# Group-norm and convolution chain, one core: statistics summed by TensorE, edge rows set by ScalarE, x1's rows stored ahead of x(2)'s loads

## Chip, cores and metric

One core of one Trainium2 chip. The metric is the device time in microseconds of one execution, median of the runs.

## What is computed

x has 8 images of 16 channels, 128 x 128, f32. Four residual steps follow each other:

```python
x = x + conv3x3(gn(x), w0) + b0                    # zero padding
x = x + newton_schulz(gn(x), 5)                    # each channel a 128x128 matrix
x = x + circular_conv3x3(gn(x), w2)                # the reference writes it with FFTs
x = x + conv3x3_cut(gn(x), K)                      # last row and column masked to 0

def gn(v, G=8, eps=1e-05):                         # 8 groups of 2 channels
    g = v.reshape(B_, G, C_ // G, H_, W_)
    m = jnp.mean(g, axis=(2, 3, 4)); s = jnp.var(g, axis=(2, 3, 4))
    return (g - m) / jnp.sqrt(s + eps)

X = W.T / (norm1 * norminf)                        # newton_schulz
for _ in range(5):
    X = X @ (2 * I - W @ X)
```

## The kernel before

The steps are called A (conv w0), B (Newton-Schulz), C (conv w2) and D (conv K).

**Convolutions.** An image is cut into NBLK = 22 windows of 8 rows x 16 channels = 128 partitions, each giving 6 output rows (96 partitions). The stationary matrix has 3 x 96 columns (one block per horizontal tap); its f32 values and those of the window are split in a high and a low fp32r part, so that a group of four windows is nine matmuls of 512 columns (`conv_group`, L815). The 22 windows are six groups (SPLIT_G). The normalization goes into the weights (1/sd, `conv_weights` L649 to L658) and into the high parts (minus the mean, ScalarE, `high_parts` L699); the low parts come from VectorE (`low_parts` L664), or from GpSimd (`low_parts_pool` L672) after ScalarE has shifted the window by L702. The output leaves PSUM by `conv_out` (ScalarE, L841).

**Statistics of a window tile** (A and D) go in four steps. `win_stats_1`: bn_stats and two bn_aggr on VectorE, one for the first 21 windows, one for the last, into mv; then `shares` (L566, L567) weights the two per partition. `win_mean` on TensorE (L710) sums over the partitions of a group with one f32 matmul of a single column against same_group. `win_stats_2` on VectorE (L602 to L631): copy of the mean, deviation, square, plus variance, `shares` again; then the values for the edges (L608), the negative mean (L609), the first window's row above the image (L614), the output's bias, the last window's row below it (L631). `win_var` (L717) sums; `win_stats_3` adds eps, ScalarE takes the root (L1026), `win_stats_4` is a reciprocal and a Newton step (L530 to L534), and `win_weights` follows. Almost every one of these operations waits for the one before it through a semaphore (class Chain). Rows B and C (the same statistics in row layout, x1 and x2) use `row_stats_1` to `row_stats_4` (L725 to L755), with `row_mean` (L760) and `row_var` (L767) on TensorE giving 16 columns, which VectorE adds in pairs (L735, L747).

**B** holds image b in x1 (128 rows x 16 channels x 128) and works on 4 channels at a time, two streams (s = 0, 1) in turn. A cycle per image has SLOTS = 24 slots; a slot is one product of a stream: TensorE (L916/L920, or L925 to L929, or L934), then ScalarE zh (L1038), then VectorE zl (L1124). Into the slots the other work is written by hand, `pe_cycle`, `act_cycle`, `dve_cycle`, `pool_cycle`, `sp_cycle`: which conv group (FILL), which step of which statistic. Cycle i computes B of image i, C of i-1, D of i-2 and A of i+3. Every engine runs its own list in order. Cycles 2 and 3 are a loop on the device, 0, 1 and 4 to 7 are written out; cycles 2, 3 and 4 are full, 5 and 6 have no A.

**Prologue.** x(0) and x(1) are loaded by three queues (every third window each: SyncE, ScalarE, GpSimd). A of 0 and 1 is done by `first_convs`; x1's rows of image 0 are gathered window by window from A's output (`rows_from_windows` L341, L345), again by the three queues. SyncE's list is: constants, taps A, x(0), taps C and D, bias, x(1), the ten loads of x(2) (L312, L317), its rows of x1, x(3), the store of x1(1) (L354); then, as cycle 0 begins, the copy x1 to x2 (L380) and the load of the next x1 (L370). VectorE's list is: stationary matrix of A, `first_convs` with x(2)'s `win_stats_1` at its end, row statistics of x1(0), the sums for B's norms (L1145, L1147), their scales, x(2)'s `win_stats_2`, the end of the row statistics, cycle 0. GpSimd forms DN (L1354) and DS (L1365), the operands of B. In cycle 0 VectorE also builds the stationary matrices of C and D (`stationary` L1216, L1223) at slots 3 to 8 (KEEP_Q).

## Time and profile before

| what | value |
|---|---|
| median of 3 runs | 738.2 us (738.06 to 3227.26) |
| profiled execution | 734.13 us, span 732.3 us |
| TensorE busy, mean granted clock | 611.9 us, 0.952 |
| VectorE, ScalarE, GpSimd busy | 538.9, 383.3, 197.7 us |

The profile is of one execution, whose own time stands beside its span. Times in it are microseconds from the span's start. PE is TensorE's matmul, PEld its weight load, DVE VectorE, ACT ScalarE, POOL GpSimd, SP SyncE; SPq, ACTq are issues of DMAs by these engines. L12 is line 12 of the kernel. The stages by their first product of a cycle: prologue to 70.5, cycles from 70.5, 150.3, 229.1, 308.0, 388.9, 467.4, 540.5 and 612.3, tail from 665.

### The profile page before, as it was taken

Reading aid. Unit: us, or ns where it says so; the run is one execution under the profiler, and the core shown is the slowest. Engines: PE = TensorE matmul, PEld = TensorE weight load, DVE = VectorE, ACT = ScalarE, POOL = GpSimd, SP = SyncE. Lnnn points to the kernel's source line nnn. Section 1 sums busy time; section 2 is a strip of 40 time slices with the busy share of each in tenths; the row PEclk is TensorE's granted clock in tenths of the full one; section 3 lists DMA queues with packets and bytes.
Section 4 is the critical chain, followed back from the end, with each engine's and each line's share of the span. In section 5 each row is a group of like instructions: output and inputs, shape, how many; then the busy total and the mean of one; then the engine's idle time right before and its main releaser. Section 6 shows DMA issues by size and latency. Waiting matters only on the chain.

```text
span 732.3 us, 11055 instructions
## 1 busy us (share of the span) xinstructions
PE 611.9 (84%) x3752; PEld 509.1 (70%) x3752; DVE 538.9 (74%) x1304; ACT 383.3 (52%) x559; POOL 197.7 (27%) x285
## 2 busy tenths in 40 slices
PE   0746788885999998989999999998979897988785
PEld 0535667775777777877877777777877787886454
DVE  4757885768688877978787968875787678856570
ACT  0430553743376745756566737673447445753472
POOL 5104222402124232512243312423032303200232
PEclk9986799998999999999999999999989998999899
DMA  6697011094049733593139614433063315134415
GB/s 171 78 116 206 7 28 55 22 193 145 30 107 97 236 87 90 74 269 77 38 87 193 174 47 102 139 121 86 18 187 101 87 38 142 66 86 121 99 48 114
DMA packets 89415, 76.52 MB, mean 104 GB/s; under 512 B 6464, under 2 KB 81568, under 8 KB 86536
## 3 DMA queue, kind: packets, MB, share of 16 engines
q1 hardware_dynamic: 84692, 72.69, 42.8%
q0 software_dynamic: 1344, 1.62, 1.1%
q10 hardware_dynamic: 3332, 1.61, 1.0%
q8 instruction: 26, 0.43, 0.3%
q14 instruction: 21, 0.17, 0.1%
HBM read 38.14 MB, written 24.25 MB: 85 GB/s over the span
## 4 chain that ended last, share of the span: by engine, by line
PE 42%; DVE 33%; ACT 9%; issue 6%; DMA 5%; SPq 3%; POOL 1%; ACTq 0%; DVEq 0%
PE conv_ps L815 23%; DVE zl L1124 7%; PE z L925 4%; PE z L934 4%; PE z L929 3%; PE z L927 3%; ACT zh L1038 3%; DVE stB L725 3%; DVE bn_D L587 2%; PE z L920 2%; DVE d_C L664 2%; ACT d_A L699 2%; DMA x<-out_C 1%; DVE bn_A L587 1%; DMA rows_dram<-x 1%
## 5 line engine op out<-in xcount | busy, mean ns | idle before, releaser
L1124 DVE SCALAR_TENSOR_TENSOR zl<-z,zh 128x1024 fp32r<-128x1024 f32 x128 | 154.4, 1219 | 77.4 <-ACT zh L1038 75.5
L925 PE MATMUL z<-zh 128*128 128x256 f32 x512 | 154.0, 301 | 12.0 <-DVE zl L1124 12.0
L1038 ACT ACTIVATE zh<-z 128x1024 fp32r<-128x1024 f32 x128 | 130.1, 1019 | 64.4 <-PE z L929 43.3
L929 PE MATMUL z<-zh,zl 128*128 128x256 f32 x512 | 147.0, 287 | 0.0
L927 PE MATMUL z<-zl,zh 128*128 128x256 f32 x512 | 147.0, 287 | 0.0
L815 PE MATMUL conv_ps<-d_C,w_C 128*96 128x512 f32 (+1 forms) x540 | 134.7, 399 | 13.8 <-POOL d_C L852 6.9
L815 PEld LDWEIGHTS conv_ps<-d_C,w_C 128*96 128x96 f32 x540 | 86.5, 172 | 43.7 <-issue 8.9
L925 PEld LDWEIGHTS z<-zh 128*128 128x128 f32 x512 | 100.4, 196 | 21.1 <-DVE zl L1124 17.7
L927 PEld LDWEIGHTS z<-zl,zh 128*128 128x128 f32 x512 | 100.3, 196 | 1.4
L929 PEld LDWEIGHTS z<-zh,zl 128*128 128x128 f32 x512 | 100.1, 195 | 0.0
L815 PE MATMUL conv_ps<-d_A,w_D 128*96 128x512 f32 (+1 forms) x378 | 91.8, 390 | 9.7 <-DVE w_D L657 9.7
L815 PE MATMUL conv_ps<-d_A,w_A 128*96 128x512 f32 (+1 forms) x378 | 89.2, 384 | 8.9 <-DVE w_A L657 7.4
L672 POOL TENSOR_TENSOR d_A<-win_D,d_A 128x512 fp32r<-128x512 f32 (+1 forms) x42 | 48.2, 1150 | 117.4 <-ACT win_D L702 117.1
L815 PEld LDWEIGHTS conv_ps<-d_A,w_D 128*96 128x96 f32 x378 | 58.7, 166 | 30.4 <-DVE w_D L657 7.4
L815 PEld LDWEIGHTS conv_ps<-d_A,w_A 128*96 128x96 f32 x378 | 58.1, 164 | 29.9 <-DVE w_A L657 6.5
L841 ACT ACTIVATE out_C<-conv_ps,col_C 96x512 f32<-96x512 f32 (+1 forms) x42 | 27.2, 648 | 65.0 <-PE conv_ps L815 64.9
L852 POOL TENSOR_TENSOR d_C<-d_C,ones_all 128x8 fp32r<-128x8 f32 (+1 forms) x96 | 22.6, 266 | 131.4 <-DVE d_C L664 131.4
L672 POOL TENSOR_TENSOR d_A<-win_A,d_A 128x512 fp32r<-128x512 f32 (+1 forms) x30 | 33.3, 1110 | 83.2 <-ACT win_A L702 83.2
L841 ACT ACTIVATE out_A<-conv_ps,col_A 96x512 f32<-96x512 f32 (+1 forms) x36 | 23.3, 648 | 58.7 <-PE conv_ps L815 58.5
L1354 POOL TENSOR_TENSOR DN<-x,tB 128x512 f32<-128x512 f32 x32 | 35.8, 1123 | 61.1 <-DVE devB L742 36.9
L841 ACT ACTIVATE out_D<-conv_ps,col_D 96x508 f32<-96x508 f32 (+1 forms) x42 | 27.1, 646 | 44.2 <-PE conv_ps L815 44.0
L1137 DVE SCALAR_TENSOR_TENSOR x<-z,sx,x 128x256 f32<-128x256 f32 x64 | 27.8, 477 | 29.5 <-PE z L934 29.5
(193 smaller groups left out, 923.1 us busy)
## 6 DMA issues: line engine op xcount, KB each, us to landing
x<-x_dram SPq DMA_DIRECT2D x14, 1024.0 KB, 7.4
win_C<-rows_dram SPq DMA_DIRECT2D x40, 256.0 KB, 4.3
rows_dram<-x SPq DMA_DIRECT2D x32, 256.0 KB
win_D<-out_C SPq DMA_DIRECT2D x7, 1056.0 KB, 6.8
y<-out_D SPq DMA_DIRECT2D x42, 168.0 KB, 3.9
win_A<-x SPq DMA_DIRECT2D x40, 160.0 KB
x_dram<-out_A SPq DMA_DIRECT2D x30, 192.0 KB, 2.4
win_D<-out_C SPq DMA_DIRECT2D x14, 160.0 KB, 5.9
```

The lines of the kernel that those rows point to most:

```text
L672: pool.tensor_tensor(c.d[:, 1, k0:k0 + kn, 1:W + 1], c.win[:, k0:k0 + kn, :], c.d[:, 0, k0:k0 + kn, 1:W + 1].bitcast(f32), ALU.subtract).t ...
L815: ins = pe.matmul(conv_ps[g % 2][0:OP, 0:kn, :], c.w[:, wp, dx * OP:(dx + 1) * OP], c.d[:, dp, k0:k0 + kn, dx:dx + W], start=n == 0, stop= ...
L841: act.activation(c.out[:, k0:k0 + kn, 0:wn], conv_ps[g % 2][0:OP, 0:kn, 0:wn], ACT.Identity, bias=col(c, OUTB, rows=OP)).then_inc(c.s_out, 1)
L852: return pool.tensor_tensor(out, in_, ones, ALU.mult)
L925: pe.matmul(z[s][:, m, :], zh[s][:, m, 0:128], zh[s][:, m, :], start=False, stop=True, skip_group_check=True)
L927: pe.matmul(z[s][:, m, :], zh[s][:, m, 0:128], zl[s][:, m, :], start=False, stop=True, skip_group_check=True)
L929: ins = pe.matmul(z[s][:, m, :], zl[s][:, m, 0:128], zh[s][:, m, :], start=False, stop=True, skip_group_check=True)
L934: ins = pe.matmul(z[s][:, m, 128:256], z4[s][:, m, 0:128], z4[s][:, m, 128:256], start=False, stop=True, skip_group_check=True)
L1038: act.activation(zh[s][:, :, :], z[s][:, :, :], ACT.Copy, scale=ROOT[j]).then_inc(s_zh[s], 1)
L1124: dve.scalar_tensor_tensor(zl[s][:, :, :], z[s][:, :, :], ROOT[j], zh[s][:, :, :].bitcast(f32), ALU.mult, ALU.subtract).then_inc(s_zl[s], 1)
L1137: ins = dve.scalar_tensor_tensor(x2[:, cs, :], z[s][:, GC * a:GC * (a + 1), 128:256], sx[:, g:g + 1], x2[:, cs, :], ALU.mult, ALU.add)
L1354: pool.tensor_tensor(DN[:, NMAT * ch:NMAT * (ch + 1), :].rearrange("p (g a) w -> p g (a w)", a=GC), x1[:, NMAT * ch:NMAT * (ch + 1), :].re ...
```

## The change

1. Sums. `shares` is gone. The constants hold four matrices minus_share (128 x 128 each, instead of one same_group and four columns); `win_mean` is two accumulating matmuls (first 21 windows, last window) and `win_var` four (variance and squared deviation of each). The results are negative, so that the negative mean comes out directly. VectorE's `win_stats_1` ends at bn_aggr; `win_stats_2` is copy, deviation, square, bias, edge values; `win_stats_4` squares and multiplies in one operation. `row_mean` is two matmuls of 8 columns and `row_var` four; VectorE's additions in pairs (L735 becomes a copy, L747 goes) and L742 go.
2. Edge rows. VectorE's L614 and L631 go; ScalarE does both inside `high_parts` (group 0 and group 5), each followed by a wait for itself.
3. Prologue, queues. SyncE: x(1) right after x(0), then the rows of x1, then x(2), x(3). Taps C, D and bias: ScalarE's queue, between x(0) and x(1).
4. Stationary matrices of C and D: by GpSimd, after its memsets and ahead of its loads of x(1), instead of VectorE in cycle 0.
5. x(2)'s statistics: `win_stats_1` after the scales of the norms; `win_stats_2`, `_3`, `_4` in slots 1, 2, 4 of cycle 0; the end of the first row statistics in slot 0; `win_mean` and `win_var` before slots 2 and 3; A2's conv groups in slots 6, 8, 9, 11, 13, 15, its high parts in 3, 4, 5, 7, 8, 10.
6. The last window of D of image 7 has no step of its own in VectorE's tail.

The core of the diff:

```diff
-K_RES = K_SEL + 128
+K_RES = K_SEL + 4 * 128
...
+    for j, share in enumerate(shares):
+        c[:, K_SEL + 128 * j:K_SEL + 128 * (j + 1)] = -share[:, None] * same_group
...
         def win_stats_2(dve, c, b):
-            link(dve.tensor_copy(col(c, MEAN), misc_ps[:, c.stat:c.stat + 1]))
+            link(dve.tensor_copy(col(c, NEG), misc_ps[:, c.stat:c.stat + 1]))
             dev2 = col(c, DEV, 2, rows=rows)
-            link(dve.tensor_scalar(dev2, c.mv[0:rows, :, 0], col(c, MEAN, rows=rows), None, ALU.subtract))
-            link(dve.tensor_tensor(dev2, dev2, dev2, ALU.mult))
-            link(dve.tensor_tensor(dev2, dev2, c.mv[0:rows, :, 1], ALU.add))
-            shares(dve, link, c, b, col(c, DEV, rows=rows), col(c, DEV + 1, rows=rows))
-            link(dve.tensor_scalar(col(c, ADD, 2), edge_drop, col(c, MEAN), None, ALU.mult))
-            link(dve.tensor_scalar(col(c, NEG), col(c, MEAN), -1.0, None, ALU.mult))
...
+            link(dve.tensor_scalar(dev2, c.mv[0:rows, :, 0], col(c, NEG, rows=rows), None, ALU.add))
+            dve.tensor_tensor(dev2, dev2, dev2, ALU.mult).then_inc(c.s_stat, 1)
+            if is_D(c):
+                dve.tensor_scalar(col(c, OUTB), col(c, NEG), -1.0, None, ALU.mult)
             else:
-                last_window(dve, c).then_inc(c.s_fix, 1)
+                dve.tensor_tensor(col(c, OUTB, rows=OP), bias[:, :], col(c, NEG, rows=OP), ALU.subtract)
+            dve.tensor_scalar(col(c, ADD, 2), minus_drop, col(c, NEG), None, ALU.mult).then_inc(c.s_fix, 1)
...
+        def edge_rows(act, c, b, k, j):
+            act.activation(c.win[:, k, :], c.win[:, k, :], ACT.Identity, bias=col(c, ADD + j),
+                           scale=edge_keep[:, j:j + 1]).then_inc(c.s_edge, 1)
+            act.wait_ge(c.s_edge, at(2, b, j + 1))
...
         def high_parts(act, c, b, g):
+            if g == 0 and not is_C(c):
+                edge_rows(act, c, b, 0, 0)
+            if g == NG - 1 and not is_C(c):
+                edge_rows(act, c, b, NBLK - 1, 1)
...
         def win_var(pe, c, b):
-            pe.matmul(misc_ps[:, c.stat + 1:c.stat + 2], same_group[0:rows, :], col(c, SUM, rows=rows),
-                      start=True, stop=True).then_inc(c.s_sum, 1)
+            out = misc_ps[:, c.stat + 1:c.stat + 2]
+            for a in range(2):
+                pe.matmul(out, minus_share[j + a][0:rows, :], c.mv[0:rows, a, 1:2], start=a == 0, stop=False)
+                ins = pe.matmul(out, minus_share[j + a][0:rows, :], col(c, DEV + a, rows=rows),
+                                start=False, stop=a == 1)
+            ins.then_inc(c.s_sum, 1)
...
         @block.sync
             load_x(sp, 0, ON_SP)
-            load_taps(sp, cC)
-            load_taps(sp, cD)
-            sp.dma_start(bias[:, :], bass.AP(tensor=b0.tensor, offset=b0.offset,
-                                             ap=[[0, OUT_ROWS], [1, C], [1, 1]])).then_inc(s_wrest, 16)
             load_x(sp, 1, ON_SP)
+            for g in range(NG):
+                rows_from_windows(sp, g, ON_SP)
             load_x_rows(sp, 2)
-            for g in range(NG):
-                rows_from_windows(sp, g, ON_SP)
             load_x_rows(sp, 3)
...
         @block.gpsimd
+            pool.wait_ge(s_cst, 16)
+            pool.wait_ge(s_wrest, 16 * 3)
+            for n, c in enumerate((cC, cD)):
+                for dy in range(TAPS):
+                    stationary(pool, c, dy, cD.scaled[:, :], s_toep_pool, (2 * TAPS - 1) * n)
             load_x(pool, 1, ON_POOL)
...
         @block.scalar
             load_x(act, 0, ON_ACT)
+            load_taps(act, cC)
+            load_taps(act, cD)
...
             load_x(act, 1, ON_ACT)
```

## Rows read from the trace of the kernel before

**Rows 1.** The page, parts 1 and 4: busy time; chain by engine.

```profile
PE 611.9 (84%) x3752; PEld 509.1 (70%) x3752; DVE 538.9 (74%) x1304; ACT 383.3 (52%) x559; POOL 197.7 (27%) x285
...
PE 42%; DVE 33%; ACT 9%; issue 6%; DMA 5%; SPq 3%; POOL 1%; ACTq 0%; DVEq 0%
```

**Rows 2.** By stage: length, busy (instructions) of engines, clock, DMA share, GB/s.

```profile
70.50:150.30 79.80, 65.29 (x391) 56.63 (x392) 59.02 (x129) 39.69 (x56) 24.92 (x23) 0.89 0.16 42
...
308.00:388.90 80.90, 74.49 (x472) 61.93 (x471) 65.52 (x160) 48.97 (x73) 24.70 (x33) 0.98 0.54 118
```

**Rows 3.** Waits of TensorE in the full cycle 308.0 to 388.9.

```profile
PE conv_ps L815 <- DVE w_D L657: 1.8, 1, 1.8
...
PE misc_ps L717 <- DVE col_A L567: 1.0, 1, 1.0
PE misc_ps L760 <- DVE stB L725: 0.8, 1, 0.8
```

**Rows 4.** Waits of TensorE in cycle 0, 70.5 to 150.3.

```profile
PE misc_ps L760 <- DVE stB L725: 3.6, 1, 3.6
...
PE conv_ps L815 <- DVE w_C L657: 2.4, 1, 2.4
```

**Rows 5.** Timeline, prologue: start, length, engine, line, operation [idle before].

```profile
39.12 0.45 ACT L841 ACTIVATE out_C<-conv_ps,col_A 96x256 f32<-96x256 f32 x1
...
40.37 1.81 DVE L664 SCALAR_TENSOR_TENSOR d_A<-win_A,col_A,d_A 128x512 fp32r<-128x512 f32 x3 [0.37 <-ACT d_A L699]
...
45.70 3.32 DVE L587 BATCH_NORM_STATS2 bn_A<-win_C 128x6 f32<-128x384 f32 x7 [3.53 <-DMA win_C<-x]
...
54.29 2.71 DVE L725 BATCH_NORM_STATS2 stB<-x 128x6 f32<-128x256 f32 x8 [4.21 <-DMA x<-out_C]
...
57.51 4.79 PE L815 MATMUL conv_ps<-d_A,w_A 128*96 128x512 f32 x18
...
76.04 2.36 DVE L1124 SCALAR_TENSOR_TENSOR zl<-z,zh 128x1024 fp32r<-128x1024 f32 x2
```

**Rows 6.** Timeline of SyncE's queue: issue start and length.

```profile
25.79 3.99 SPq L312 DMA_DIRECT2D win_C<-x  x8
...
31.48 11.99 SPq L341 DMA_DIRECT2D x<-out_C  x7
43.51 0.70 SPq L345 DMA_DIRECT2D x<-out_C  x1
44.27 10.33 SPq L312 DMA_DIRECT2D win_A<-x  x8
...
68.49 0.37 SPq L370 DMA_DIRECT2D x<-x_dram  x1
```

**Rows 7.** A stretch of four microseconds, columns as in rows 2.

```profile
30.00:34.00 4.00, 4.00 (x21) 2.95 (x20) 2.27 (x13) 1.27 (x2) 1.75 (x3) 1.00 1.28 113
```

**Rows 8.** The view of DMAs: one issue, KB each, us to landing.

```profile
y<-out_C POOLq DMA_DIRECT2D x7, 48.0 KB, 3.0
```

**Rows 9.** The page, part 5: GpSimd's smallest tensor_tensor, mean ns second.

```profile
L852 POOL TENSOR_TENSOR d_C<-d_C,ones_all 128x8 fp32r<-128x8 f32 (+1 forms) x96 | 22.6, 266 | 131.4 <-DVE d_C L664 131.4
```

**Rows 10.** Timeline beside GpSimd's DS; durations of L566, min/median/max.

```profile
69.40 1.08 DVE L604 TENSOR_SCALAR col_A<-mv_A,col_A 128x2 f32<-128x2 f32 x1
69.42 4.04 POOL L1365 TENSOR_TENSOR DS<-DN,scl 128x512 f32<-128x512 f32 x4 [6.71 <-DVE scl L1165]
...
L566 DVE TENSOR_TENSOR col_A<-col_A,cst x8: 158/160/962, 17.8 to 434.6; 128x1 f32<-128x1 f32 x8
```

**Rows 11.** Groups by line: busy us, mean ns.

```profile
L614 DVE TENSOR_SCALAR win_D<-win_D,cst,col_D 128x128 f32<-128x128 f32 x7 | 2.4, 346 | 0.9 <-DVE col_D L609 0.8
...
L1223 DVE TENSOR_TENSOR base_C<-base_C,scaled_C 128x288 f32<-128x288 f32 x2 | 1.8, 899 | 0.1
...
L1216 DVE TENSOR_TENSOR scaled_C<-compact_C,cst 128x288 f32<-128x288 f32 x2 | 0.9, 448 | 0.0
```

**Rows 12.** Timeline of TensorE's weight loads.

```profile
349.82 0.50 PEld L916 LDWEIGHTS z<-cst,DS 128*128 128x128 f32 x4
```

More of the change, by code:

```diff
@@ L111, in build @@
         ident = cst[:, K_IDENT:K_IDENT + 128]
-        same_group = cst[:, K_SEL:K_SEL + 128]
-        share = cst[:, K_SHARE:K_SHARE + 4]
+        minus_share = [cst[:, K_SEL + 128 * j:K_SEL + 128 * (j + 1)] for j in range(4)]
         residual = cst[:, K_RES:K_RES + WN]
@@ L616, in win_stats_2 @@
-            if is_tail(c, b):
-                first.then_inc(s_first, 1)
-            if not is_D(c):
-                link(dve.tensor_tensor(col(c, OUTB, rows=OP), col(c, MEAN, rows=OP), bias[:, :], ALU.add))
-            else:
-                link(dve.tensor_copy(col(c, OUTB), col(c, MEAN)))
-            if is_tail(c, b):
-                dve.wait_ge(s_first, 1)
-                dve.memset(col(c, SPARE), 0.0).then_inc(c.s_fix, 1)
-            else:
-                last_window(dve, c).then_inc(c.s_fix, 1)
+            link(dve.tensor_scalar(dev2, c.mv[0:rows, :, 0], col(c, NEG, rows=rows), None, ALU.add))
@@ L1219, in stationary, with dve_cycle @@
                 tap_mask[:, dy, :].unsqueeze(1).unsqueeze(3).broadcast_to([128, TAPS, OUT_ROWS, C]),
[L1220 to L1221 removed]
+                ALU.mult).then_inc(done, 1)
+            eng.wait_ge(done, n)
             if dy:
[L1223 to L1226 removed]
+                eng.tensor_tensor(base, base, tmp, ALU.add).then_inc(done, 1)
+                eng.wait_ge(done, n + 1)
+        def dve_cycle(dve, i, has_D, has_C, has_A, nxt, load, first_link_B=None):
             for q in range(SLOTS):
                 dve_slot(dve, i, q)
[L1229 to L1233 removed]
                 if has_C and q == 1:
```

180 lines of the change are left out of this document (83 added, 97 removed).

## The prediction

> **What bounds the kernel now.** I read the page's head first, then the busy time by stage, then, stage by stage, the timeline and who waits. The head says that TensorE is busy for 84% of the span and VectorE for 74%, and that the chain that ended last runs 42% on TensorE and 33% on VectorE [rows 1]. No engine is the bound everywhere, so the stages have to be taken singly. The table by stage [rows 2] shows two kinds. In a full cycle (308.0 to 388.9) TensorE is busy 74.5 of 80.9 us, VectorE 65.5, ScalarE 49.0: TensorE is nearly full. Its waits there are few and short, and each ends with a product of VectorE: 1.8 us for D's weights, 1.0 for the sum of the second statistics, 0.8 for the row statistics [rows 3]. So there a microsecond of TensorE work costs up to a microsecond, and VectorE work is worth only what it takes off these waits. Cycle 0 (70.5 to 150.3) holds 65.3 us of TensorE work in 79.8 at a granted clock of 0.89; its waits are longer, 3.6 us for row statistics and 2.4 for A2's weights [rows 4].
>
> The prologue, 0 to 70.5, is bound by neither. VectorE has the low parts of x(1) done at 42.2 (40.37 + 1.81), takes x(2)'s statistics from 45.70, and then idles until 54.29, when x1's rows have landed [rows 5]. The queue of SyncE says why: the ten loads of x(2) are issued from 25.79, the rows of x1 after them, seven issues that take 12 us because the queue is full, and the last at 43.51 [rows 6]. ScalarE had that last group ready at 39.6 (39.12 + 0.45) [rows 5]. The queue moved 113 GB/s then [rows 7].
>
> **Part 1: x1's rows ahead of x(2).** SyncE has nothing before the rows, so the last is issued at about 39.7. Its landing took 10.8 us in the loaded queue (43.51 to 54.29); a transfer of the same 48 KB in a quiet stretch takes 3.0 [rows 8]. I take 3.0, since the queue is now empty, and keep 10.8 as the far end. Rows at 43 instead of 54.29 is 11.3 us. TensorE then does not stand idle before the row mean, so its last two conv groups run at full clock (some 3.4 us where they took 4.79 [rows 5]); but it is busy to 46.9 first. It finishes x(1) at 46.9 + 0.6 + 3.4 = 50.9 instead of 62.3: 11.4 earlier, and norms, scales and the first product z follow at that distance.
>
> Before, VectorE reached the first zl only at 76.04 [rows 5], 1.6 us after its zh, because the second statistics of x(2) and the end of the row statistics stood ahead. These move into slots 0 and 1; in their place stand x(2)'s first statistics, 4.2 us (seven of 3.3 together [rows 5] and a tail of 0.9). VectorE would be free at 57.9 + 4.2 = 62.1, and zh is there at 63.0. So the first zl comes 13.0 us earlier, if x(2) has landed by 58. It is issued at 41; 1.39 MB at 113 GB/s is 12.3 us, and it lands near 55. So it is there in time, with 3 us to spare; beyond that each microsecond would count.
>
> **Part 2: what is put ahead of x(0) and x(1).** The constants grow from 289 to 479 KB in front of x(0)'s windows: at some 200 GB/s 0 to 1 us, and x(1)'s loads are now less in the way; I take 0.5. The taps of C and D and the bias move from SyncE's queue to ScalarE's, behind x(0) in both. VectorE needs the bias at about 16, as before.
>
> GpSimd now builds the stationary matrices of C and D: ten operations of 288 elements, once these taps are there, at 12 to 15 us. Not shown in this trace; from both sides: its 128x8 operation takes 0.27 us [rows 9], its 128x512 one 1.01 (four in 4.04 [rows 10]). By size between them, 0.68 each, 7 us in all, until about 22. They collide twice. First, x(1)'s seven loads by GpSimd are queued behind them: issued from 22 instead of 6.4, the last lands near 29.5, and x(1)'s statistics ran from 25.7 to 29.2; that costs 0 to 3 us. Second, x(0)'s statistics run on VectorE at the same time. While GpSimd has a tensor_tensor, small operations of VectorE are held up: L604 took 1.08 us beside DS, and L566 shows 0.16 as its median and 0.96 as its longest [rows 10]. Three or four such operations on x(0)'s path are each held for 0.5 us (0.68 less their own 0.16): 1.5 to 2. The shorter chain gives back 0.5. The two do not add, since the later decides. Together with the constants I take 2 us (0 to 5), which leaves 11 of the 13.
>
> The Trainium skill, in "SBUF — State Buffer", section "SBUF: two separate sides", says that VectorE and GpSimd hold one pair of ports exclusively for a whole instruction. L604 agrees: it ended with GpSimd's first operation. By that rule every two-input operation would wait for a whole 0.68, some eight of them 4 us instead of 2, and the sum would be 2 us worse.
>
> **Part 3: cycle 0.** VectorE loses ten stationary steps: six multiplications of 0.45 and four additions that were held up (C's two averaged 0.90) [rows 11], 6.1 us in all, the greater part before the row statistics for which TensorE waited 3.6 us. A2's convolution starts in slot 6 instead of 4, so the 2.4 us for its weights should go too [rows 4]. A later A2 group also fills TensorE at slot 13, before the second sum of A. What is late next is VectorE's moved second statistics (some 2.5 us at slots 0 and 1, where it idled 2.6 us for zh) and x1's second image, below. Cost 0 to -7; I take -4.
>
> The queue pays for part 1: x(2), x(3), x1's store, the copy x1 to x2 and the load of x1(1) were issued from 25.79 to 68.49, and now begin at 41. They are 6.0 MB. The load of x1(1) then lands at about 83 + the 2 us, and VectorE wants it in slot 5, at about 83 + 2 as well. I take nothing, with 0 to 3 for the range.
>
> **Part 4: statistics in every cycle.** A sum of statistics was one f32 matmul, which the trace shows as two passes. Means become two matmuls, variances four: 2 and 6 passes more, 8 for each of the four statistics of a full cycle (A, D, and rows of B and C), so 32. A pass of one column is bound by its weights: four f32 loads of 128 columns took 0.50 us, the last of them 0.14, so 0.11 to 0.12 apart [rows 12]. That is 3.5 us of TensorE time a cycle; over all 32 statistics 256 passes, 28 us. Bounds: 0.03 a pass (a load that was hidden) and 0.21 at the half clock.
>
> Against it stand VectorE's savings: two edge operations of 0.35 (L614's row and L631's equal) [rows 11], two of each of L566 and L567, L606, L609 and one Newton step, 1.9 us without holds for a window statistic; two operations, 0.35, for a row one. ScalarE gets the two edge rows instead: 128 elements each, where 256 take 0.45 [rows 5]; I take 0.33 (0.1 to 0.45) and 0.07 for its wait for itself, 0.4, with high_parts, zh and the square root queued behind.
>
> In the full cycle, by TensorE's waits [rows 3]: C's rows +0.9, of which the 0.8 us wait for stB takes nearly all, +0.1; B's rows +0.9, less 0.6 of two short waits; A's mean +0.2; A's second sum is reached 0.3 earlier and has 0.7 more passes, +0.4 (its wait was 1.0); A's weights: 0.4 edge less 0.2 Newton, +0.2; D's mean and variance +0.9 less 0.3; D's weights +0.1. Sum +1.9, and I take 1.7 for the holds that VectorE no longer suffers. Bounds -1 and +3.5. Three full cycles: +5. Cycle 1 waits much more for VectorE, and the late cycles have no A: +1.5 over the four. In the tail conv D of image 6 waits 2.2 us for its weights behind a VectorE chain of these operations: -1.5.
>
> **The sum.** -11 (prologue) -4 (cycle 0) +5 (cycles 2 to 4) +1.5 -1.5 = -10. The profiled execution took 734.1 us (span 732.3): it becomes 724.1. The median of the runs is 738.2, 4.1 above it; on that scale 728.2 us.
>
> **Rivals.**
> Steady cycles stay as they are: the holds and the shortened chains pay for the passes (VectorE has 33% of the chain, and loses some 45 us outside the stationary steps by my count). For it: each wait of TensorE in the full cycle ends with VectorE; against: they sum to only 6 us. Then -15 or, with a fuller prologue, -17: 721.
>
> The passes come on top (the one that ends slower): TensorE in the cycles, no wait absorbing, 256 x 0.11 = 28 us, less the 15 of prologue and cycle 0: +13, 751. For it: TensorE is at 92% of the full cycle [rows 2]; against: by the same view of waits, cycle 1 has 12 us of them and each late cycle 8, nearly all for VectorE. It decides as soon as more than 15 us of the 28 stay.
>
> The load path gives the prologue back: GpSimd's ten operations cost 5 us ahead of x(0) and x(1), and x1(1) comes 3 us late in slot 5. Then -10 + 3 + 3 = -4: 734. For it: the holds of [rows 10]; against: x1's path has 11 us to win.
>
> The rows land no earlier: if the landing of 10.8 us was the transfer's own and not the queue's, only the issue counts, 3.8 us, and the sum is -3: 735. A 3.0 us landing of the same size speaks against it [rows 8].
>
> **Chances.** Forecast 0.45 (its own range 723 to 733); steady cycles unchanged 0.25; passes on top 0.12; load path 0.13; rows no earlier 0.05. Two per cent, 14.8 us, is about what a measurement of this kernel can tell from no change. Faster by more: the second case's greater part and the edge of the first, 0.28. Slower by more: the far part of the third, 0.06. Within: 0.66. The range 717 to 741 takes in the second case and half the third.
>
> **What would show it.** Right: stB's first operation at 43 to 47 and the first zl at 63 to 67; no wait above 1 us for stB in cycle 0; full cycles 1 to 3 us longer with TensorE's busy time 3 to 4 us up and VectorE's down by 5; L604's class held up at 16 to 22. Wrong: a first zl later than 70; VectorE waiting for a load of x in slot 5 or before x(2)'s statistics; full cycles no longer than 79, or over 83.

## The result, and the profile after

The change takes 728.84 us (median; lowest 726.79, highest 735.26) where the kernel before takes 738.13 beside it: ratio 0.990 (95% interval 0.986 to 0.994), 1.0% faster, which is inside the 2% that count as no change. One of the four executions of the kernel before took 3227 us; its median isn't moved by it. Repeated later with more runs the change is at 729.38 us, ratio 0.987 (0.984 to 0.991). The forecast was 728.2, within 2%. The total came out; several of its terms did not, and this section and the next ones take them apart.

A first trap. The two profiled executions run against the medians: 735.26 us (span 733.5) after, 734.13 (span 732.3) before. The execution of before that was profiled is 4 us below its median, that of after 6 above its own. So each kernel was profiled a second time: before again has a span of 739.4, after again 732.3.

The head and the chain of the page of the kernel after:

```profile
span 733.5 us, 11366 instructions
...
PE 631.9 (86%) x4008; PEld 533.1 (73%) x4008; DVE 496.1 (68%) x1109; ACT 398.7 (54%) x591; POOL 203.1 (28%) x295
...
PE 52%; DVE 16%; ACT 10%; SPq 8%; DMA 6%; issue 5%; POOL 1%; ACTq 1%; DVEq 0%
```

Against [rows 1]: TensorE is busy for 20.0 us more, although its mean granted clock is higher (0.969 for 0.952), VectorE for 42.8 less. VectorE's share of the chain halved, 33% to 16%, and TensorE's rose by 10 points; SyncE's issues and DMAs took another part (3% and 5% became 8% and 6%). Work left the engine that waited and was put on the one that was nearly full.

The busy time by stage (columns as in [rows 2]), the stages cut at the first product of each cycle: prologue, cycles 0 to 6, cycle 7 with the tail:

```profile
0.00:61.98 61.98, 34.23 (x164) 25.52 (x164) 36.69 (x96) 18.37 (x32) 26.22 (x48) 0.99 0.61 106
61.98:140.94 78.96, 66.00 (x417) 57.47 (x418) 51.16 (x114) 41.51 (x60) 24.35 (x23) 0.92 0.40 83
140.94:223.24 82.30, 71.18 (x467) 61.71 (x466) 57.51 (x128) 42.23 (x60) 18.09 (x28) 0.94 0.52 110
...
304.29:385.36 81.07, 76.08 (x504) 64.50 (x503) 60.63 (x136) 50.63 (x76) 24.54 (x34) 1.00 0.53 118
...
465.86:536.55 70.69, 64.22 (x437) 55.80 (x436) 50.31 (x110) 38.18 (x53) 18.36 (x27) 0.99 0.36 105
536.55:610.90 74.35, 66.35 (x436) 57.73 (x436) 51.92 (x111) 39.88 (x56) 18.50 (x27) 0.96 0.34 96
610.90:733.50 122.60, 101.60 (x591) 81.37 (x590) 66.69 (x146) 66.63 (x103) 23.92 (x45) 0.95 0.34 93
```

The lengths of these stages in both kernels, cut in the same way in each trace (us):

| stage | before | before again | after | after again |
|---|---|---|---|---|
| prologue | 70.5 | 75.9 | 62.0 | 61.8 |
| cycle 0 | 79.8 | 78.9 | 79.0 | 78.5 |
| cycle 1 | 78.8 | 81.3 | 82.3 | 83.0 |
| cycles 2, 3, 4 | 79.0, 80.9, 78.5 | 79.0, 80.9, 78.6 | 81.1, 81.1, 80.5 | 81.1, 81.1, 80.5 |
| cycle 5 | 73.1 | 73.1 | 70.7 | 70.7 |
| cycle 6 | 71.7 | 71.7 | 74.4 | 74.4 |
| cycle 7 and tail | 120.1 | 120.0 | 122.6 | 121.2 |

The prologue is the gain, 8.5 us against the first profile and 13.9 against the second. From cycle 1 on all but cycle 5 gives back: +3.5, +2.1, +0.2, +2.0, -2.4, +2.6, +2.5, against the first profile of before. The +3.5 of cycle 1 is +1.0 against the second, where that cycle took 81.3.

The prologue's timeline in the kernel after:

```profile
42.47 0.46 ACT L841 ACTIVATE out_C<-conv_ps,col_A 96x256 f32<-96x256 f32 x1
...
42.95 0.70 SPq L346 DMA_DIRECT2D x<-out_C  x1
...
43.70 4.06 SPq L313 DMA_DIRECT2D win_C<-x  x8
...
46.68 2.71 DVE L722 BATCH_NORM_STATS2 stB<-x 128x6 f32<-128x256 f32 x8 [0.94 <-DMA x<-out_C]
...
49.53 12.89 SPq L313 DMA_DIRECT2D win_A<-x  x8
...
62.16 3.32 DVE L581 BATCH_NORM_STATS2 bn_A<-win_C 128x6 f32<-128x384 f32 x7 [1.36 <-DMA win_C<-x]
...
66.01 1.19 DVE L1127 SCALAR_TENSOR_TENSOR zl<-z,zh 128x1024 fp32r<-128x1024 f32 x1
```

The last rows of x1 are issued the moment ScalarE has them, 42.95, and land 3.7 us later, where the same bytes took 10.8 behind x(2). The first zl begins at 66.01, not 76.04 [rows 5]. In the second profile of before these two rows are later still:

```profile
58.81 2.71 DVE L725 BATCH_NORM_STATS2 stB<-x 128x6 f32<-128x256 f32 x8 [7.72 <-DMA x<-out_C]
...
81.42 2.36 DVE L1124 SCALAR_TENSOR_TENSOR zl<-z,zh 128x1024 fp32r<-128x1024 f32 x2
```

The same instructions, 4.5 and 5.4 us later in another execution of the same kernel. Of the 4.5, 2.0 are a later issue (45.56 for 43.51) and 2.5 a longer landing (13.3 for 10.8), so the profile on which the prediction rests had an early one. In the two profiles of the kernel after, that step begins at 46.68 both times, 3.7 and 3.9 us after the issue.

### The profile page after: what moved, and what is told of

Read it like the earlier page. It is cut to its first block, busy times and chain, and to the rows that moved or that the text cites. A ratio compares the mean times of both kernels' runs of the same rounds, so it can differ in the third digit from the quotient of the medians.

```text
span 733.5 us, 11366 instructions
## 1 busy us (share of the span) xinstructions
PE 631.9 (86%) x4008; PEld 533.1 (73%) x4008; DVE 496.1 (68%) x1109; ACT 398.7 (54%) x591; POOL 203.1 (28%) x295
## 3 DMA queue, kind: packets, MB, share of 16 engines
q1 hardware_dynamic: 84318, 72.74, 42.8%
## 4 chain that ended last, share of the span: by engine, by line
PE 52%; DVE 16%; ACT 10%; SPq 8%; DMA 6%; issue 5%; POOL 1%; ACTq 1%; DVEq 0%
PE conv_ps L815 26%; PE z L924 5%; PE z L926 4%; PE z L928 4%; DVE zl L1127 4%; PE z L933 3%; ACT zh L1041 3%; SPq L313 3%; PE z L919 2%; ACT d_A L690 2%; DMA win_C<-rows_dram 2%; PE spare_ps L944 1%; DVE stB L722 1%; DMA rows_dram<-x 1%; DMA win_D<-out_C 1%
## 5 line engine op out<-in xcount | busy, mean ns | idle before, releaser
L815 PE MATMUL conv_ps<-d_C,w_C 128*96 128x512 f32 (+1 forms) x540 | 133.6, 396 | 15.6 <-POOL d_C L852 8.2
L924 PEld LDWEIGHTS z<-zh 128*128 128x128 f32 x512 | 99.1, 194 | 17.8 <-DVE zl L1127 14.6
L815 PE MATMUL conv_ps<-d_A,w_D 128*96 128x512 f32 (+1 forms) x378 | 88.8, 380 | 10.0 <-DVE w_D L642 10.0
L815 PEld LDWEIGHTS conv_ps<-d_A,w_D 128*96 128x96 f32 x378 | 57.1, 162 | 29.8 <-DVE w_D L642 8.3
L1349 POOL TENSOR_TENSOR DN<-x,tB 128x512 f32<-128x512 f32 x32 | 35.7, 1119 | 42.9 <-DVE devB L737 23.7
```

What stands on the lines that cost most here:

```text
L815: ins = pe.matmul(conv_ps[g % 2][0:OP, 0:kn, :], c.w[:, wp, dx * OP:(dx + 1) * OP], c.d[:, dp, k0:k0 + kn, dx:dx + W], start=n == 0, stop= ...
L924: pe.matmul(z[s][:, m, :], zh[s][:, m, 0:128], zh[s][:, m, :], start=False, stop=True, skip_group_check=True)
L1349: pool.tensor_tensor(DN[:, NMAT * ch:NMAT * (ch + 1), :].rearrange("p (g a) w -> p g (a w)", a=GC), x1[:, NMAT * ch:NMAT * (ch + 1), :].re ...
```

## Experiments

Each is an edit of the kernel after, apart from the repeats. Ratios are to the kernel before on the same chip, whose medians were 737.9 to 738.5 us throughout.

**The kernels themselves again.** No edit.

> The changed kernel as it is, run again beside the kernel before. My theory (prologue 8 to 10 us shorter, full cycles 2 us longer each) puts it 8 to 11 us below the kernel before, and a second profile of it should show the full cycles at 80.5 to 81.1 us again and cycle 1 or 6 shorter than the 82.3 and 74.4 of the first profile, if those two are only scatter between executions. The rival, that the cycles 1 and 6 are really 3 us longer, expects the same 82 and 74 again.

Measured: 729.38 us, 0.987 (0.984 to 0.991); stages in the table above. Cycles 1 and 6 came at 83.0 and 74.4 again, as the rival had it. Cycle 1 of before moves by 2.5 us between its own two profiles, though, so only cycle 6 is settled by this.

> The kernel before as it is, for a second profile and for the scatter of the method. Ratio 1 within 0.4%. The full cycles stay at 78.5 to 79.0 us (80.9 in the one with the loop's end) in every profile; only cycle 0 and the prologue may differ, with TensorE's granted clock.

Measured: 738.55 us, 1.001 (0.998 to 1.004), span of the profiled execution 739.4. What follows: the cycles of before agree between its two profiles within 0.1 us from cycle 2 on; only prologue, cycle 0 and cycle 1 move.

**Queue order undone.** x1's rows behind x(2) again.

```diff
             load_x(sp, 1, ON_SP)
+            load_x_rows(sp, 2)
             for g in range(NG):
                 rows_from_windows(sp, g, ON_SP)
-            load_x_rows(sp, 2)
```

> The changed kernel with one part undone: SyncE issues x(2)'s ten loads ahead of its rows of x1 again. Theory: the rows land late again, so the first row statistics begin near 56 us instead of 46.7 and the whole is 8 to 10 us slower than the changed kernel, that is, equal to the kernel before within 2 us. Rival (the rows' landing time was the transfer's own, not the queue's): 3 to 4 us slower than the changed kernel. Second rival (the prologue's gain comes from taking x(2)'s statistics out of VectorE's way): 0 to 2 us slower.

Measured: 735.9 us, 0.996 (0.994 to 0.998): 6.5 slower than the change, between the theory (8 to 10) and its first rival (3 to 4). Row statistics begin at 52.7 instead of 46.7 (the landing took 8.3 us) and the first zl at 74.0 instead of 65.8, 8.2 later; cycle 0 is then 75.0 instead of 78.5. The order of one queue is the largest single part of the gain, and not all that it gains at the first zl is still there at the end.

**Stationary matrices undone, and later.** One kernel gives them back to VectorE in slots 3 to 8 of cycle 0:

```diff
-                    stationary(pool, c, dy, cD.scaled[:, :], s_toep_pool, (2 * TAPS - 1) * n)
...
+                if is_int(i, 0) and 3 <= q < 9:
+                    step = q - 3
+                    stationary(dve, (cC, cD)[step // TAPS], step % TAPS, cD.scaled[:, :], s_toep,
+                               (2 * TAPS - 1) * (1 + step // TAPS))
```

The other leaves them with GpSimd, but behind its loads:

```diff
-            pool.wait_ge(s_cst, 16)
-            pool.wait_ge(s_wrest, 16 * 3)
-            for n, c in enumerate((cC, cD)):
-                for dy in range(TAPS):
-                    stationary(pool, c, dy, cD.scaled[:, :], s_toep_pool, (2 * TAPS - 1) * n)
             load_x(pool, 1, ON_POOL)
             for g in range(NG):
                 rows_from_windows(pool, g, ON_POOL)
+            pool.wait_ge(s_cst, 16)
+            pool.wait_ge(s_wrest, 16 * 3)
+            for n, c in enumerate((cC, cD)):
+                for dy in range(TAPS):
+                    stationary(pool, c, dy, cD.scaled[:, :], s_toep_pool, (2 * TAPS - 1) * n)
```

> The changed kernel with the ten stationary steps of C and D back on VectorE in slots 3 to 8 of cycle 0; the taps are loaded as in the changed kernel. Theory: first convolution at 22.5 to 23.5 instead of 24.5, the first zl at least 1 us earlier unless x(2)'s landing holds it; cycle 0 then 3 to 5 us longer, because VectorE's 6 us of steps stand before the row statistics for which TensorE waits; 1 to 4 us slower than the changed kernel. Rival (VectorE has room in cycle 0 now, its second statistics having lost their holds): the prologue's gain alone, 1 to 2 us faster.

Measured: 732.14 us, 0.991 (0.988 to 0.994): 2.8 slower than the change, with intervals that overlap. Its first convolution is at 24.59, not at the 22.5 to 23.5 expected, and its cycle 0, 79.2 us, is 0.8 longer than that of after again, not 3 to 5.

> The changed kernel with GpSimd's ten stationary steps moved behind its loads of x(1) and its rows of x1, just ahead of DN. Theory: the small operations of VectorE on x(0)'s path are no longer held up (L597, L602, L627, L640, L641 were 0.4 to 0.5 us longer each), so the first convolution starts 2 us earlier, at 22.8 instead of 24.85; but DN may wait for the tenth step by 0 to 1 us, and x(2)'s landing, which already ended the wait for its statistics, moves with it. 1 to 2 us faster than the changed kernel. Rival (the prologue is bound by x(2)'s landing or by the load queues, not by this chain): the same within 0.5 us.

Measured: 728.31 us, 0.986 (0.982 to 0.989): 1.1 faster than the change, and the intervals overlap. The 22.8 expected for the first convolution was missed as well. First GpSimd's and VectorE's timelines of the kernel after, where they collide:

```profile
15.35 0.67 POOL L1217 TENSOR_TENSOR base_C<-compact_C,cst 128x288 f32<-128x288 f32 x1 [8.70 <-DMA bias<-b]
...
17.73 0.69 POOL L1217 TENSOR_TENSOR scaled_D<-compact_C,cst 128x288 f32<-128x288 f32 x1
...
23.68 2.40 POOL L331 DMA_DIRECT2D win_A<-x  x4 [0.30 <-POOL base_D L1224]
```

```profile
14.42 0.56 DVE L581 BATCH_NORM_STATS2 bn_A<-win_C 128x6 f32<-128x384 f32 x1 [0.29 <-DMA win_C<-x]
...
17.02 0.65 DVE L597 TENSOR_SCALAR col_A<-mv_A,col_A 128x2 f32<-128x2 f32 x1
...
17.79 0.64 DVE L602 TENSOR_TENSOR col_A<-bias,col_A 96x1 f32<-96x1 f32 x1
...
20.26 0.16 DVE L624 RECIPROCAL col_A<-col_A 128x1 f32<-128x1 f32 x1 [0.27 <-ACT col_A L1029]
...
21.03 0.65 DVE L627 TENSOR_TENSOR col_A<-col_A 128x1 f32<-128x1 f32 x1
21.71 1.02 DVE L640 SCALAR_TENSOR_TENSOR scaled_C<-base_A,col_A,cst 128x288 f32<-128x288 f32 x1
```

L602, one element a partition, runs from 17.79 to 18.43, and GpSimd's operation from 17.73 to 18.42. And the kernel with the steps later:

```profile
15.94 0.56 DVE L581 BATCH_NORM_STATS2 bn_A<-win_C 128x6 f32<-128x384 f32 x1 [0.94 <-DMA win_C<-x]
...
18.54 0.23 DVE L597 TENSOR_SCALAR col_A<-mv_A,col_A 128x2 f32<-128x2 f32 x1
18.88 0.15 DVE L602 TENSOR_TENSOR col_A<-bias,col_A 96x1 f32<-96x1 f32 x1
...
21.99 0.16 DVE L627 TENSOR_TENSOR col_A<-col_A 128x1 f32<-128x1 f32 x1
22.19 0.52 DVE L640 SCALAR_TENSOR_TENSOR scaled_C<-base_A,col_A,cst 128x288 f32<-128x288 f32 x1
...
24.35 3.27 PE L815 MATMUL conv_ps<-d_C,w_C 128*96 128x512 f32 x7 [3.46 <-DVE d_C L649]
```

The holds are gone (L597 0.65 to 0.23, L602 0.64 to 0.15, L640 1.02 to 0.52). But the first convolution still starts at 24.35, against 24.85 and 24.53 in the two profiles of the change. x(0)'s last window is there at 15.94 instead of 14.42: GpSimd, no longer held by the ten steps, issues x(1)'s loads at 6.43 and not at 23.68, and x(0) shares the transfers with them. Undoing the steps altogether gives the same (last window 16.2, convolution 24.59). The ten steps delayed VectorE by 2 us and, by holding x(1)'s loads back, brought x(0) in 1.5 us sooner. The profiles of all changed kernels fall into two groups: in the seven with the steps ahead the last window comes at 14.0 to 14.4 and the convolution 10.3 to 11.2 us after it, in the five others at 15.9 to 16.2 and 7.8 to 8.4 after it. In the two of before, with smaller constants in front, it came at 14.6 and 15.6.

The same pair shows cycle 0. Its granted clock (the third column from the right), in stretches of 6 us, in the second profile of the change and then with the steps later:

```profile
84.00:90.00 6.00, 4.50 (x29) 4.25 (x28) 5.93 (x14) 2.93 (x4) 1.63 (x2) 0.82 0.14 34
...
96.00:102.00 6.00, 3.75 (x30) 3.46 (x29) 2.07 (x4) 1.97 (x4) 1.88 (x3) 0.95 0.13 33
102.00:108.00 6.00, 6.00 (x35) 5.06 (x34) 2.07 (x4) 0.74 (x2) 0.01 (x1) 0.76 0.03 8
```

```profile
84.00:90.00 6.00, 4.89 (x35) 4.30 (x34) 5.89 (x12) 3.96 (x5) 1.77 (x2) 1.00 0.14 34
...
96.00:102.00 6.00, 3.75 (x26) 3.07 (x26) 3.58 (x8) 0.54 (x2) 1.68 (x2) 1.00 0.13 33
102.00:108.00 6.00, 6.00 (x44) 5.13 (x42) 3.06 (x4) 2.96 (x4) 2.08 (x2) 1.00 0.37 120
```

In the full 6 us of 102 to 108 TensorE does 35 matmuls at 0.76 and 44 at 1.00. Cycle 0 lasts 75.0 us where the clock held and 78.5 and 79.0 where part of it ran at the lower of the two levels (1.2 GHz). TensorE is idle for 2.25 of the 6 us from 96 to 102 in both, and for 1.5 and 1.1 from 84 to 90; why the clock fell in one and not in the other isn't settled, and the medians differ by 1.1 us alone. The other executions of the change point the same way: four of its ten have a mean clock of 0.969 to 0.971 and take 729.7 to 735.3 us, the profiled two among them, and six have 0.975 to 0.977 and take 726.8 to 730.4. So the two profiles probably show what cycle 0 costs when the clock falls in it, and most executions of the change are without that; none of those was profiled.

**Sums undone.** `shares` and the pairwise additions back on VectorE, one matmul for each sum.

```diff
-            dve.tensor_tensor(dev2, dev2, dev2, ALU.mult).then_inc(c.s_stat, 1)
+            link(dve.tensor_tensor(dev2, dev2, dev2, ALU.mult))
+            link(dve.tensor_tensor(dev2, dev2, c.mv[0:rows, :, 1], ALU.add))
+            shares(dve, link, c, b, col(c, DEV, rows=rows), col(c, DEV + 1, rows=rows))
...
-            for a in range(2):
-                pe.matmul(out, minus_share[j + a][0:rows, :], c.mv[0:rows, a, 1:2], start=a == 0, stop=False)
-                ins = pe.matmul(out, minus_share[j + a][0:rows, :], col(c, DEV + a, rows=rows),
-                                start=False, stop=a == 1)
-            ins.then_inc(c.s_sum, 1)
+            pe.matmul(out, minus_share[0][0:rows, :], col(c, SUM, rows=rows),
+                      start=True, stop=True).then_inc(c.s_sum, 1)
```

> The changed kernel with its sums of statistics back on VectorE: one matmul for each sum, shares and pairwise additions as before; edges, queues and slots stay changed. Theory: 256 passes fewer on TensorE take about 2 us off each full cycle and 1 off the others, VectorE's longer chains cost little; 4 to 8 us faster than the changed kernel, full cycles near 79.5. Rival (sums for nothing: the shorter VectorE chain pays for the passes): within 2 us of it. Rival (the passes come wholly on top): 20 to 28 us faster.

Measured: 723.54 us, 0.979 (0.975 to 0.983): 5.8 faster than the change. The full cycle:

```profile
296.18:376.01 79.83, 73.03 (x471) 60.85 (x470) 63.56 (x150) 50.24 (x77) 24.85 (x33) 1.00 0.55 120
```

TensorE 3.0 us less busy than after, VectorE 2.9 more, the cycle 1.2 shorter. The other 1.8 us are waits that are longer without the change: for D's weights 1.8 instead of 1.3, for A's second sum 1.0 instead of 0.4, for zl 1.0 instead of 0.6, for the sums of the norms 0.5 instead of 0.2.

**Edges undone.** Both edge rows back on VectorE.

```diff
+            first = dve.tensor_scalar(c.win[:, 0, :], c.win[:, 0, :], edge_keep[:, 0:1], col(c, ADD),
+                                      ALU.mult, ALU.add)
...
+                last_window(dve, c).then_inc(c.s_fix, 1)
...
-            if g == 0 and not is_C(c):
-                edge_rows(act, c, b, 0, 0)
-            if g == NG - 1 and not is_C(c):
-                edge_rows(act, c, b, NBLK - 1, 1)
```

> The changed kernel with its edge rows back on VectorE (and the tail's own step for the last window of D). Theory, from the full cycles of the run with the sums undone (1.0 us shorter, of the 2.1 by which the changed kernel's are longer): the other 1.1 us is the two extra operations and their self-waits on ScalarE ahead of high_parts and of the square root. So the full cycles become 80.0 us, and the whole 4 to 7 us faster than the changed kernel. Rival (ScalarE has room, being busy for 54%, and VectorE gains by it): full cycles unchanged or longer, the whole the same or 2 us slower.

Measured: 721.98 us, 0.979 (0.976 to 0.982): 7.4 faster than the change. The total is what was expected and the place isn't: in the full cycles it is worth only 0.3, 0.3 and 0.9, where the theory had 1.1 in each; the rest is outside them, in cycle 0 (75.7 us, 2.8 less than after again), cycle 1 (79.7, 3.3 less), cycle 6 (71.8, 2.6 less) and cycle 7 with the tail (118.6, 2.6 less), with cycle 5 1.7 longer. These differences are of two profiled executions 12.1 us apart, where the medians are 7.4 apart, so not all of them are the edit's. Cycle 6 can be read off: with both parts it is 73.9 to 74.5 in five profiles and 77.4 in a sixth, without one of them or both 71.1 to 72.1 in all. The chain in the second profile of the change:

```profile
605.22 1.88 SPq L427
...
607.14 3.37 DMA win_D<-out_C
...
610.61 0.50 ACT win_D L609
...
611.14 0.72 ACT d_A L690
611.86 0.61 ACT win_D L693
612.47 0.10 ACT col_D L1029
...
616.51 1.65 PE conv_ps L815 x6
```

The edge row (L609, 0.50 us) waits for D's window to land and is followed on ScalarE by a high part, the shift of the window and only then the square root, L1029; the weights wait for the root. TensorE waits 2.7 us for them. In the kernel before that wait is 0.8 and the one for D's mean 3.0; the change cuts the latter to 1.3 in cycles 5 and 6 alike. Cycle 5, whose window lands in time, keeps that (w_D 1.1, the cycle 2.4 shorter, part of it by a granted clock of 0.99 where before has 0.94), and cycle 6 does not. Either undoing, sums or edges, gives 71.9 or less: it takes both parts to make 74.4.

**More passes.** Four more matmuls ahead of each second sum, into columns that nothing reads: work added, nothing else changed.

```diff
             out = misc_ps[:, c.stat + 1:c.stat + 2]
+            for a in range(2):
+                pe.matmul(misc_ps[:, 200:201], minus_share[j + a][0:rows, :], c.mv[0:rows, a, 1:2],
+                          start=a == 0, stop=False)
+                pe.matmul(misc_ps[:, 200:201], minus_share[j + a][0:rows, :], col(c, DEV + a, rows=rows),
+                          start=False, stop=a == 1)
```

> The changed kernel with four more f32 matmuls ahead of each second sum, into a scratch column: 256 passes of TensorE more, as many as the change added. They are extra work only. Theory: 0.11 us a pass in a packed stretch, of which the full cycle's waits take up a part: full cycles 2 to 3 us longer, the whole 10 to 18 us slower. Rival (the passes hide in TensorE's waits): full cycles under 1 us longer, the whole under 5 us. Rival (all on top): 3.5 us a full cycle, 28 us in all.

Measured: 757.43 us, 1.025 (1.023 to 1.028): 28.0 us slower than the change for 256 passes (32 sums, four matmuls, two passes each), 0.11 us a pass. That is the price in the prediction and in the second rival (all on top), against a theory of 10 to 18 us. Full cycles last 86.1, 84.6 and 85.5 us, 5.1, 3.6 and 5.0 more than the change's for 32 passes each. In the middle one the granted clock is 1.00 and no wait is shorter: 3.6 us for 32 passes is 0.11 each, wholly on top. In the other two it is 0.98, and the lower level costs them 1.5 more. Cycle 6 is 0.4 shorter than the change's, since its wait of 2.7 for D's weights is gone: there the passes were absorbed. The page has 4264 matmuls where the change has 4008.

**Sums and edges both undone:** the diffs of the two put together, which leaves queues, slots and GpSimd's matrices; and the same with the matrices later, as above.

> The changed kernel with both sums and edge rows back on VectorE; what remains of the change is the prologue's queues, GpSimd's stationary steps and x(2)'s slots. If the costs of sums and edges add, full cycles are back at the 78.5 to 79.0 us of the kernel before and the whole is 10 to 12 us faster than the changed kernel, near 717. Rival (they overlap: VectorE, given both back, becomes the bound): full cycles 80 us, no faster than the better of the two single undoings, 722 to 724.

Measured: 720.03 us, 0.976 (0.974 to 0.979).

> As the kernel with both sums and edges back, and GpSimd's stationary steps just ahead of DN as well. Theory: first convolution 0.5 us and first zl 0.3 us earlier as in the run with the steps moved alone; 0 to 1 us faster than without the move. Rival: VectorE's longer chain in the prologue (sums and edges back on it) meets the moved steps elsewhere: up to 2 us slower.

Measured: 717.89 us, 0.974 (0.972 to 0.977). The full cycle is back at 78.9 (queues alone):

```profile
293.27:372.14 78.87, 72.90 (x471) 60.87 (x470) 64.62 (x154) 48.65 (x72) 24.69 (x33) 1.00 0.56 121
```

Sums and edges together cost 9.4 us of the whole (729.4 less 720.0), just short of the 10 to 12 expected, 2.2 us in each full cycle, all at a granted clock of 1.00. Singly undone they give 5.8 and 7.4, 13.2, so they overlap: put on alone, the sums cost 2.0 (722.0 less 720.0) and the edge rows 3.5 (723.5 less 720.0; the intervals overlap in both), and the rest of the 9.4 is there only with both, as in cycle 6.

**Only the slots.** With sums and edges undone, the queue order and the stationary matrices undone as well: the four diffs above put together.

> What remains of the change when the sums, the edge rows, the queue order and the stationary steps are all undone: x(2)'s statistics and A2's groups in their later slots, the taps on ScalarE's queue. The single undoings (order 6.5 us, stationary steps 2.8, sums and edges together -9.4) leave about 9 us of the distance to the kernel before that none of them explains. Theory: it is in the slots, x(2)'s second statistics no longer standing before the first zl with GpSimd's DS holding up each of their operations, and A2's groups filling TensorE's waits; then this kernel is 5 to 9 us faster than the kernel before, with z0 to the first zl at 4 us instead of 5.5. Rival: it is interaction of the parts (each of order and stationary steps is worth more when the other is undone): within 2 us of the kernel before.

Measured: 732.8 us, 0.992 (0.989 to 0.994): 5.1 us below before. Its first zl is at 77.25, between the two of before, 3.9 us after the first product of its cycle where before has 5.5 twice, and its cycle 0 is 77.4 (79.8 and 78.9 before). Another 2.0 are in cycle 3, 78.8 for 80.9, far from any slot that moved. The kernel is not quite the slots alone: the edit for the sums doesn't give back two operations for each window statistic, one of the Newton step and one in `win_stats_2`, and the larger constants and the taps in ScalarE's queue stay too. The remaining 12.8 us to the kernel with the queues (720.0) are the order and the matrices.

**Half of the sums.** Window statistics: the weighting by TensorE (two matmuls for the mean, two for the variance), the variance added to the squared deviation by VectorE. Row statistics and edges as before the change; matrices later.

```diff
-            dve.tensor_tensor(dev2, dev2, dev2, ALU.mult).then_inc(c.s_stat, 1)
+            link(dve.tensor_tensor(dev2, dev2, dev2, ALU.mult))
+            dve.tensor_tensor(dev2, dev2, c.mv[0:rows, :, 1], ALU.add).then_inc(c.s_stat, 1)
...
-                pe.matmul(out, minus_share[j + a][0:rows, :], c.mv[0:rows, a, 1:2], start=a == 0, stop=False)
                 ins = pe.matmul(out, minus_share[j + a][0:rows, :], col(c, DEV + a, rows=rows),
-                                start=False, stop=a == 1)
+                                start=a == 0, stop=a == 1)
```

> The queues and the late stationary steps, edge rows on VectorE, row statistics as before, and of the windows' sums only the weighting on TensorE: two matmuls for each mean and each variance, the variance and the squared deviation added on VectorE. 8 passes more in a full cycle instead of 32, and VectorE's longest-held operation (the shares) gone. Theory (a pass costs 0.11 us on top, what VectorE sheds is worth about as much): within 2 us of the kernel with all sums on VectorE, 716 to 720. Rival (the holds of VectorE were worth more): 3 us or more faster than it.

Measured: 714.62 us, 0.968 (0.965 to 0.971): the best of all, 23 us under before and 15 under the change. The full cycle:

```profile
292.33:371.12 78.79, 73.57 (x479) 61.85 (x478) 63.33 (x146) 48.69 (x72) 24.68 (x34) 1.00 0.55 122
```

Beside the same row of the kernel with sums and edges undone: TensorE 0.7 us more, VectorE 1.3 less, and the cycle as long, 78.8 for 78.9. The nearest kernel to compare is the one with the matrices later, 0.974 against 0.968, on another chip; the intervals just part, and 1.7 us of the 3.3 stand in cycles 5 and 6 (72.1 and 71.1 for 73.1 and 71.8). So weighting by TensorE is worth some 3 us, as the rival had it, and the rest of the sums on TensorE costs more than that: with the edge rows on VectorE, as here, all of them were 2.0 slower than none, and with the edge rows on ScalarE 5.8.

## Why the prediction was right, and where it was not

**Part 1, the rows ahead.** Right in place and size of the first zl: -11 forecast, 10.0 measured against the profile used (15.4 against the second). The last issue was put at 39.7, 41.7 with the 2 us of part 2, and came at 42.95; the landing was put at 3.0 and was 3.7. One step was wrong: x(2) "lands near 55", with "3 us to spare" (its own terms, 41 and 12.3, give 53). It was issued at 43.70 and VectorE could start on it at 62.16, 18.4 us later. The rows of before had the better figure: the same ten loads, issued from 25.79 [rows 6], were there at 45.70 [rows 5], 19.9 us. In both kernels other transfers are issued right behind them, x1's rows before and x(3)'s ten loads now; from 44 to 62 all queues together moved about 2 MB, of which x(2) is 1.39, and the sum had given x(2) the whole rate. That those behind take a share fits both, but no run leaves them out. It cost almost nothing: first statistics to 66.0, zh ready at 65.9. The rival in which the rows land no earlier is out.

**Part 2, GpSimd's steps.** "Three or four such operations ... 1.5 to 2": six are held (L597, L602, L625, L627, L640, L641), and without them the chain from x(0)'s statistics to its convolution is 2.0 us shorter. The steps last 0.67 to 0.89 and end at 23.4, not 22; between 0.27 for 128 elements and 1.01 for 512 the size gives 0.58, and the prediction's 0.68 came nearer by luck. But that term of the sum is not what they cost, since their absence lets x(1)'s loads take x(0)'s rate: the net at the first convolution is 0.2 to 0.9 us (24.85 and 24.53 against 24.35; 25.08 against 24.18 with sums and edges undone). The prediction had priced GpSimd's late loads only as a loss for x(1).

The Trainium skill's rule in "SBUF — State Buffer", section "SBUF: two separate sides", that VectorE and GpSimd hold a pair of ports for a whole instruction, agrees with the rows: L602 ends 0.01 us after GpSimd's operation. What is not held is L624, a reciprocal of one input, 0.16 us in the middle of a GpSimd operation (20.11 to 20.79).

**Part 3, cycle 0.** Forecast -4; -0.8 and -1.3 in the two profiles of the change, -4.8 in the one where the clock held. The waits:

```profile
PE spare_ps L944 <- DVE sums L1150: 3.5, 2, 2.3
PE conv_ps L815 <- DVE w_C L642: 2.3, 1, 2.3
PE misc_ps L755 <- DVE stB L722: 2.1, 1, 2.1
```

"The 2.4 us for its weights should go too" is wrong: 2.3 are still there (against [rows 4]), probably since x(2)'s second statistics moved with the convolution. "No wait above 1 us for stB" is wrong as well: 3.6 became 2.1. The wait for the sums of the norms grew to 3.5 (0.4 and 1.1 before), which no term had, and the load of x1(1) was late by 0.9 us, for which nothing had been taken. The -4 came out only where the clock held, and the prediction had no term for the clock.

**Part 4, the passes.** +5 forecast for three full cycles. Against the kernel before it is +4.3 (2.1, 0.2, 2.0), against the kernel with sums and edges undone +6.6 (2.2 in each), with TensorE busy 3.2 more and VectorE 4 less. The second is the cleaner pair, because cycle 3 of before, from which the prediction took its rows, is itself 2.0 us longer than its neighbours, in both profiles:

```profile
312.67 3.77 PE L815 MATMUL conv_ps<-d_A,w_D 128*96 128x512 f32 x9 [1.83 <-DVE w_D L657]
```

```profile
314.00:316.00 2.00, 2.00 (x6) 1.31 (x5) 2.00 (x5) 0.00 (x0) 0.00 (x0) 0.50 1.23 182
```

Two of VectorE's operations ahead of D's weights stood beside GpSimd's and were long (L531 0.57, L655 1.39 where cycle 2 has 0.20 and 0.52), TensorE waited 1.8 us for the weights instead of 1.4, its granted clock then fell to the lower level, and the nine matmuls took 3.77 instead of 2.36. In none of the changed kernels is cycle 3 more than 0.1 us longer than cycle 2. With the sums undone the wait is 1.8 too and the clock holds, so what tips it is open. The change, then, also took 2.0 us off that cycle without a term in the sum, and the passes and edge rows cost 2.2 there as in the others, 0.5 more than forecast.

The working behind the size is not right either. It had let C's row wait for stB swallow 0.8 of 0.9. TensorE's waits in the full cycle after:

```profile
PE conv_ps L815 <- DVE w_A L642: 1.6, 1, 1.6
PE conv_ps L815 <- DVE w_D L642: 1.3, 1, 1.3
PE misc_ps L755 <- DVE stB L722: 0.8, 1, 0.8
```

The stB wait is the same 0.8 as in [rows 3]: passes that stand behind a wait don't shorten it. The wait for A's weights is that of before too:

```profile
PE conv_ps L815 <- DVE w_A L657: 1.6, 1, 1.6
```

It is 1.6 as well with the edge rows undone, so the 0.2 for them ahead of A's root isn't seen in a full cycle. What paid part of the passes was VectorE: by the price measured with more passes, 256 of them are 28 us, and undoing the sums gives back 5.8, or 2.0 where the edge rows are VectorE's. Some 22 to 26 us were therefore saved, a difference of runs and not itself a measurement. The rival "passes come on top" had the price right, and its deciding point, 15 of 28 us kept, was not reached.

**The other cycles and the tail.** +1.5 for cycles 1, 5, 6 and 7, and -1.5 for the tail, together 0: measured +6.3 in the first profile (+3.5, -2.4, +2.6, +2.5), and +3.7 against the second of before. This is the step that failed most. Cycle 5 had the only gain of the kind that the sum expected (the mean of D). Cycle 6 is the edge row ahead of the root. In cycle 1 TensorE waits 6.2 us for stB (5.6 and 8.2 in the two of before), and the chain there begins with a transfer, the window of C landing at 161.31, after which ScalarE's high part (161.41, 0.72), zh, zl and the row statistics follow in turn. But the kernel with sums and edges undone waits 6.1 us there too, and its cycle 1 is 79.3: TensorE is busy 4.0 us less in it and has 32 matmuls fewer, so the passes, for which the sum took little here, fit the 3.0 us between the two better than the transfer does. In the tail the wait for D's weights did fall from 2.2 to 0.9, as forecast, but C's window landed after 7.16 us instead of 4.91 and TensorE waited 8.2 for GpSimd's padding instead of 6.9. Whether the landing is the change's doing or that execution's is open: after again has 1.4 us less there. The 0.4 us for an edge row was 0.50, and its price is not its time but the queue behind it: 7.4 us in all for the 16 window statistics with the sums on TensorE (3.5 without), where the sum had the queue behind it as a remark.

**The two scales.** The sum put the profiled execution at 724.1 and added 4.1 for the median. The profiled execution of the change came at 735.3, and the other three of that measurement at 726.8 to 730.4; the clock explains part (mean 0.969 against 0.975 to 0.977). In medians, the parts are: slots -5.1, queue order and matrices -12.8, sums and edges +9.4, that is -8.5. The sum's +5 for sums and edges was too low by some 4, and its -15 for the rest too small by 3: two errors that cancel. That the total came within a microsecond of the forecast is luck to that extent. The parts were measured on different chips, with intervals of about 2 us to each side, so each is good to a few microseconds.

## What to carry to other kernels

Move work to another engine only from a wait that it ends: here the order of one queue and ten steps on an idle engine brought 12.8 us, while moving sums from an engine at 74% to one at 84% put 28 us of passes on it to get back 22 to 26. A small f32 matmul has the price of its weight loads (two here, 0.11 us each), so fold one weighting into it where it takes a chain of tiny operations away, and leave plain additions where they are. An instruction with a wait that is put ahead of others on an in-order engine costs what is queued behind it, and its own microsecond is the smaller part.

## What the runs showed of the hardware beyond the forecast

- A transfer lands later than its bytes at the queue's rate when others are issued around it: x(2), ten loads of 1.39 MB, took 18.4 us with x(3)'s ten right behind and 19.9 with x1's rows behind, where 113 GB/s gives 12.3. x(0)'s last window came 1.5 us later when GpSimd issued x(1) at 6.4 instead of 23.7.
- A landing at the end of a loaded queue differs widely: x1's last rows took 8.3 to 13.3 us from issue to first use in four profiles (10.8 and 13.3 in the two of one kernel). At the head of an empty one it was 3.7 to 5.0 in ten.
- The lower clock level comes in cycle 0 in some executions and not in others of nearly the same kernel: 78.5 against 75.0 us.
